# Spreading side work and reordering products around two pairs of attention outputs

## The chip, the cores and the metric

The kernel runs on one core of a Trainium2 chip. The metric is the time of one execution on the device in microseconds (us), as the median of several runs. The engines are TensorE (PE in the rows), VectorE (DVE), ScalarE (ACT), GpSimd (POOL) and SyncE (SP), which here only starts transfers.

## The reference

Four sequences `x` of 512 x 512 go through two layers. All is float32.

```python
q, k, v = x @ Wq, x @ Wk, x @ Wv
attn_out = (softmax(q @ k.T * scale) @ v) @ Wp + bp
cms_out = gelu(attn_out @ cW1 + cb1) @ cW2 + cb2 + one_hot(target_codes)
modifier = gelu(concat(attn_out, cms_out) @ mW1 + mb1) @ mW2 + mb2
x = clip(x + cms_out + modifier, 0, 1)
h = gelu(x @ W_down[stream] + b_down[stream]) @ W_up[stream] + b_up[stream]
out = layernorm(x + h) * ln_w[stream] + ln_b[stream]
```

`cW1` is 512 x 2048, `mW1` 1024 x 2048, `cW2` and `mW2` 2048 x 512. Each sequence picks one of three adapters (`W_down` 512 x 256, `W_up` 256 x 512).

## The kernel before

**Numbers in two parts.** Every matrix is split into a `hi` part (ScalarE copies it rounded) and a `lo` part (value minus `hi`, on VectorE or GpSimd), and each product is three matmuls: hi x hi, lo x hi, hi x lo (L727, L728, L729). Each matmul moves 512 columns.

**Attention** fills the first part of the time, a batch at a time. Its outputs are kept as operands: `xo[0]` for batches 0 and 1, `xo[1]` for batches 2 and 3. The two-layer perceptrons multiply 2 x 2 blocks with seven products in place of eight (the Strassen-Winograd scheme), so each pair of batches gives seven operands: the blocks `B11`, `B21`, `B22` and the sums `T1` to `T4`. Each has a `_hi`, a `_lo` and a float tile `_f` of 128 x 1024; in the trace their names are shown without the numbers, `x_B_hi`, `x_T_lo`, `x_T_f` and so on. `c_B` and `c_T` are those made from `cms_out` (`co[0]`, `co[1]`).

**Groups.** 32 groups g follow. Groups 0 to 15 are the first perceptron (`cW1`, `cW2`), with the pair of batches alternating; groups 16 (`MOD0`) to 31 are the second (`mW1`, `mW2`), 16 to 23 for batches 0 and 1, 24 to 31 for 2 and 3. A group has seven products i = 0 to 6, with operands B11, T2, T1, B21, T3, T4, B22, in three banks. Below group 16 a product has 6 matmuls; from 16 on it has 12, 6 with attention operands (`left_x`) and 6 with `cms_out` operands (`left_c`). Products 3 to 6 go on in a bank that holds an earlier one, so they wait until it has been read: product 3 for ScalarE's `keep_first` (bank 0 to `s1_t`, L1052), product 4 for VectorE's `join` U2, product 5 for U3, product 6 for JC22 (L1337). Then `gelu` (L1046) makes the four blocks C11, C22, C21, C12 of `H_hi` and `gelu_low` (L1325) those of `H_lo`. `out_tiles(g, h)` multiplies them by the second weights in four tiles of 6 matmuls each, in four further banks, and `add_outputs` (VectorE, L1348, L1352, L1354) adds these to `acc`. TensorE's order in a group g is: products 0, 1, `out_tiles(g-1, 0)`, products 2, 3, 4, `out_tiles(g-1, 1)`, products 5, 6. In group 16 it is: the attention parts of products 0, 1, 2, both `out_tiles(15, ...)`, the `cms_out` parts of 0, 1, 2, then 3 to 6. `out_tiles(g, 0)` needs `gelu_low` of C21, which the order on VectorE puts after those of C11 and C22, and `out_tiles(g, 1)` that of C12.

**Operands on their way.** `left` tiles are made from `rawX` and `rawC` (loads by SyncE, sums on GpSimd, `left_hi` on ScalarE, `left_lo` on GpSimd), `second_hi` and `second_lo` make the second weights (`W_hi`, `W_lo`, L962, L552). A left tile i is written anew after product i of the group has been made. Every engine works through its own list in order.

**Around the change.** After attention VectorE makes T2, T3, T4 of pair 1 as three differences (L1279) and, in group 0, the `lo` parts of T2, T1, T3 (L1293), while GpSimd makes those of B11, B21, T4, B22. In group 2 SyncE stores all fourteen `xo[1]` tiles of 512 KB to DRAM (L459). In groups 2 to 13 the adapters are split in 24 pieces of 128 x 256, two in each group: `split_piece` on SyncE (L412, L415) loads one, waits for the split and stores it before it goes on; ScalarE's `piece_to_hi` (L1056) stands ahead of `gelu` of C11, and a second time behind that of C22. In group 15 and 16 the `co[0]` operands are made, in 23 and 24 the `co[1]` ones (`co_sum` L1279, `co_hi` L1030, `co_lo` L1298 on VectorE and L552 on GpSimd); in group 23 `x1_home` and `cms_home` bring pair 1 back (L430, L434).

## Time and profile before

| | us |
|---|---|
| median of 3 runs | 1136.68 |
| lowest and highest | 1136.36, 1138.86 |
| the profiled execution's own time | 1140.68 |
| its span, first to last instruction | 1138.4 |
| TensorE busy in it | 1077.0 (95%) |
| mean granted TensorE clock | 0.982 of full |

The time of an execution holds 2.3 us more than its span. TensorE is busy nearly all the time; the rest of the span is its idle time, and some stretches of its busy time have a lower granted clock.

### The profile page before, as it was taken

What the parts mean: (1) busy time and instruction counts of PE and PEld (TensorE: products, weight loads), DVE (VectorE), ACT (ScalarE), POOL (GpSimd) and SP (SyncE); (2) the same over time, 40 slices, a digit from 0 to 9 for tenths busy, and PEclk for the clock granted to TensorE, in tenths of its full rate; (3) what the DMA queues carried; (4) which work ended last, traced back from release to release, by engine and by line L of the source; (5) the groups of instructions that cost most, each with busy time, mean ns of one, the idle gap of its engine ahead of it and who ended that gap; (6) DMA issues with size and microseconds to landing.
All of it is one profiled execution on the core that took longest, in us unless ns stands there. A gap on an engine that the chain in (4) does not pass through costs nothing.

```text
span 1138.4 us, 13134 instructions
## 1 busy us (share of the span) xinstructions
PE 1077.0 (95%) x4736; PEld 884.8 (78%) x4736; DVE 602.5 (53%) x831; ACT 458.2 (40%) x870; POOL 549.8 (48%) x561
## 2 busy tenths in 40 slices
PE   7999999787899999999988999999889999999996
PEld 6888888566678778778867888888678888888885
DVE  3634344562655555555663455554575455455567
ACT  3524345431433433433444333343523344332665
POOL 0501155640432422432577666666887666663414
PEclk9999999989999999999999999999989999999999
DMA  7301000107221221121041112222834212213733
GB/s 259 129 2 37 16 22 20 37 1 282 70 70 56 60 70 56 61 70 42 19 139 47 65 65 65 65 65 71 344 115 145 65 65 65 66 65 139 277 102 121
DMA packets 62064, 100.51 MB, mean 88 GB/s; under 512 B 5680, under 2 KB 35376, under 8 KB 61488
## 3 DMA queue, kind: packets, MB, share of 16 engines
q1 hardware_dynamic: 61424, 98.62, 25.3%
q10 hardware_dynamic: 576, 1.05, 0.2%
q8 instruction: 38, 0.62, 0.2%
q14 instruction: 26, 0.21, 0.1%
HBM read 77.63 MB, written 22.02 MB: 88 GB/s over the span
## 4 chain that ended last, share of the span: by engine, by line
PE 84%; DVE 7%; ACT 2%; issue 2%; SPq 2%; DMA 2%; POOL 1%; ACTq 0%; DVEq 0%
PE bank L727 28%; PE bank L728 28%; PE bank L729 28%; SPq L459 1%; DVE c_T_f L1279 1%; DVE z L1447 1%; DMA c_B_f<-cms_kept 1%; DVE x_T_lo L1293 1%; DVE stats L1441 1%; PE bank L771 1%; DVE c_T_lo L1298 1%; POOL left_c L552 1%; DMA piece_raw<-adapter_dram 0%; POOL W_lo L552 0%; ACT acc L1076 0%
## 5 line engine op out<-in xcount | busy, mean ns | idle before, releaser
L727 PE MATMUL bank<-H_hi,W_hi 128*128 128x512 f32 x512 | 201.9, 394 | 15.5 <-issue 9.3
L552 POOL TENSOR_TENSOR left_x<-rawX,left_x 128x256 fp32r<-128x256 f32 x144 | 126.5, 879 | 163.0 <-ACT left_x L957 162.7
L729 PE MATMUL bank<-H_hi,W_lo 128*128 128x512 f32 x512 | 200.9, 392 | 0.0
L728 PE MATMUL bank<-H_lo,W_hi 128*128 128x512 f32 x512 | 200.7, 392 | 0.0
L1354 DVE TENSOR_TENSOR acc<-bank,acc 128x512 f32<-128x512 f32 x224 | 151.1, 687 | 90.6 <-PE bank L729 90.2
L1337 DVE TENSOR_TENSOR u_t<-bank,s_t 128x512 f32<-128x512 f32 x64 | 44.2, 691 | 159.4 <-PE bank L729 157.3
L727 PEld LDWEIGHTS bank<-H_hi,W_hi 128*128 128x128 f32 x512 | 97.3, 190 | 38.8 <-issue 15.2
L957 ACT ACTIVATE left_x<-rawX 128x256 fp32r<-128x256 f32 x144 | 58.1, 411 | 151.2 <-DMA rawX<-mW_dram 76.8
L727 PE MATMUL bank<-x_T_hi,left_x 128*128 128x512 f32 x256 | 101.2, 395 | 12.6 <-DVE u_t L1337 11.1
L729 PEld LDWEIGHTS bank<-H_hi,W_lo 128*128 128x128 f32 x512 | 97.0, 189 | 20.7
L728 PEld LDWEIGHTS bank<-H_lo,W_hi 128*128 128x128 f32 x512 | 97.3, 190 | 20.1
L1046 ACT ACTIVATE H_hi<-u_t,bias 128x512 fp32r<-128x512 f32 x64 | 45.9, 718 | 147.7 <-PE bank L729 137.9
L729 PE MATMUL bank<-x_T_hi,left_x 128*128 128x512 f32 x256 | 100.4, 392 | 0.0
L728 PE MATMUL bank<-x_T_lo,left_x 128*128 128x512 f32 x256 | 100.4, 392 | 0.0
L552 POOL TENSOR_TENSOR piece_lo<-piece_raw,piece_hi 128x256 fp32r<-128x256 f32 x24 | 17.7, 737 | 145.0 <-ACT piece_hi L1056 145.0
L1325 DVE TENSOR_TENSOR H_lo<-u_t,H_hi 128x512 fp32r<-128x512 f32 x64 | 70.8, 1106 | 24.6 <-ACT u_t L1046 24.6
L727 PE MATMUL bank<-x_B_hi,left_x 128*128 128x512 f32 x192 | 75.7, 395 | 6.8 <-ACT gelu_f L1046 6.8
L729 PE MATMUL bank<-x_B_hi,left_x 128*128 128x512 f32 x192 | 75.4, 393 | 0.0
L728 PE MATMUL bank<-x_B_lo,left_x 128*128 128x512 f32 x192 | 75.4, 393 | 0.0
L552 POOL TENSOR_TENSOR left_c<-rawC,left_c 128x256 fp32r<-128x256 f32 x96 | 74.2, 773 | 2.4 <-ACT left_c L957 2.4
L727 PEld LDWEIGHTS bank<-x_T_hi,left_x 128*128 128x128 f32 x256 | 48.3, 189 | 25.9 <-DVE u_t L1337 13.0
L552 POOL TENSOR_TENSOR xn_lo<-x_raw,xn_hi 128x512 fp32r<-128x512 f32 x16 | 21.0, 1319 | 96.6 <-ACT xn_hi L985 96.6
(184 smaller groups left out, 2329.2 us busy)
## 6 DMA issues: line engine op xcount, KB each, us to landing
rawX<-mW_dram SPq DMA_DIRECT2D x16, 512.0 KB, 3.4
rawC<-mW_dram SPq DMA_DIRECT2D x16, 512.0 KB, 5.1
W_raw<-mW_dram SPq DMA_DIRECT2D x16, 512.0 KB, 3.7
xT_raw<-xT_dram SPq DMA_DIRECT2D x4, 1024.0 KB, 8.5
x_raw<-x_dram SPq DMA_DIRECT2D x4, 1024.0 KB, 6.4
rawX<-cW_dram SPq DMA_DIRECT2D x8, 512.0 KB, 3.6
W_raw<-cW_dram SPq DMA_DIRECT2D x8, 512.0 KB, 4.0
out_dram<-z SPq DMA_DIRECT2D x16, 256.0 KB, 2.0
```

The source lines that it names most:

```text
L459: sp.dma_start(x1_kept[i, half], f32(flat(xo[1][i][half][:, :, :]))).then_inc(x1_saved, 16)
L552: pool.tensor_tensor(dst, src, f32(hi), ALU.subtract).then_inc(done, 1)
L727: pe.matmul(tile, sh, mh, start=first_one and n == 0, stop=False, skip_group_check=joined_group)
L728: pe.matmul(tile, sh, ml, start=False, stop=False, skip_group_check=joined_group)
L729: last = pe.matmul(tile, sl, mh, start=False, stop=last_one and n == len(terms) - 1, skip_group_check=joined_group)
L771: last = pe.transpose(bank_of(n)[:, cols(c)], prob[:, t, cols(c)], ident[:, :])
L957: act.activation(left(s, i)[0], left_source(s, i), ACT.Copy).then_inc(A_hi_made[s], 1)
L1046: act.activation(dst, src, ACT.Gelu, bias=bias[:, column:column + 1]).then_inc(gelu_made, 1)
L1279: dve.tensor_tensor(dst[2][:, :, :], a, b, ALU.subtract).then_inc(done, 1)
L1325: dve.tensor_tensor(H_lo[:, c, :], f[:, :], f32(H_hi[:, c, :]), ALU.subtract).then_inc(gelu_lo_made, 1)
L1337: dve.tensor_tensor(dst[:, :], bank[b][:, :], other[:, :], ALU.add).then_inc(joined, 1)
L1354: op = dve.tensor_tensor(dst, src, dst, ALU.add)
```

## The change

- **Pair 1.** All `lo` parts of `xo[1]` move to VectorE, and none is left on GpSimd. B11's comes between the attention bias additions; T2's difference after them; T4's difference after U2 of group 0, T2's `lo` after JC22, T3's difference at the end of group 0; in group 1 the `lo` parts of T1 and B21 come between U2 and `add_outputs(0, 0)`, those of T3, T4, B22 behind it. ScalarE makes T3's and T4's `hi` between `gelu` C21 and C12 of group 0.
- **Order.** Groups 0 and 16 make product 4 ahead of product 3 (`order_of`).
- **Pieces.** One a group, in groups 3 to 26; `split_piece` is cut in `load_piece`, early in SyncE's list for the group, and `save_piece`, at its end (in group 23 it stands ahead of `x1_home(5)` and `x1_home(6)`); `piece_to_hi` and `piece_split` move to the end of the group, ahead of `second_hi` and `second_lo` there.
- **Stores.** Two of the fourteen `xo[1]` stores in each of groups 4 to 10.
- **Group 16.** All `co_lo(0, ...)` but B11 and B21 on VectorE; `add_outputs(15, ...)` earlier among them; `second_hi` right after `gelu` C11 and `second_lo` ahead of `left_lo(..., 2)`.
- **Group 24.** `co_lo(1, T2)` moves up into group 23, before `add_outputs(22, 1)`; T1's and T3's behind `add_outputs(23, 0)`.
- **Warm.** One Gelu on a 128 x 1 tile in attention's last batch.

```diff
@@ -136,6 +136,7 @@
...
+        warm = sm("warm", [1])
...
@@ -282,8 +283,11 @@
...
+        def order_of(g):
+            return (0, 1, 2, 4, 3, 5, 6) if g in (0, MOD0) else range(7)
+
         def products(g, i):
-            return 7 * g + i + 1
+            return 7 * g + list(order_of(g)).index(i) + 1
...
@@ -345,10 +349,11 @@
...
-        PIECE_GROUPS = range(2, 2 + PIECES // 2)
+        PIECE_GROUPS = range(3, 3 + PIECES)
...
         XO_HI_ORDER = (T1, T2, T3, T4)
+        XO_SUM_ORDER = [(T2, T3, T4), (T2, T4, T3)]
...
@@ -405,11 +410,13 @@
...
-            def split_piece(u):
-                e, part = u // PARTS, u % PARTS
+            def load_piece(u):
                 if u > 0:
                     sp.wait_ge(piece_saved, 32 * u)
-                sp.dma_start(piece_raw[:, :], adapter[e, part]).then_inc(piece_loaded, 16)
+                sp.dma_start(piece_raw[:, :], adapter[u // PARTS, u % PARTS]).then_inc(piece_loaded, 16)
+
+            def save_piece(u):
+                e, part = u // PARTS, u % PARTS
                 sp.wait_ge(piece_lo_made, u + 1)
                 for half, tile in enumerate((piece_hi, piece_lo)):
                     sp.dma_start(experts[e, half, :, 256 * part:256 * (part + 1)], f32(tile[:, :])).then_inc(piece_saved, 16)
@@ -452,22 +459,23 @@
...
-                if g == 2:
-                    for i in range(7):
-                        sp.wait_ge(xo_made[1][i], 1)
-                        for half in range(2):
-                            sp.dma_start(x1_kept[i, half], f32(flat(xo[1][i][half][:, :, :]))).then_inc(x1_saved, 16)
                 if g in PIECE_GROUPS:
-                    split_piece(2 * (g - 2))
+                    load_piece(g - 3)
+                if 4 <= g < 11:
+                    i = g - 4
+                    sp.wait_ge(xo_made[1][i], 1)
+                    for half in range(2):
+                        sp.dma_start(x1_kept[i, half], f32(flat(xo[1][i][half][:, :, :]))).then_inc(x1_saved, 16)
                 if g % 2 == 0 and g // 2 + 1 < 8:
                     load_second(g // 2 + 1)
                 if g in PIECE_GROUPS:
-                    split_piece(2 * (g - 2) + 1)
+                    save_piece(g - 3)
 
             for g in range(MOD0, GROUPS):
                 sets = splits_in(g)
                 if g == MOD0:
                     load_left(*sets[0])
+                    load_piece(g - 3)
...
@@ -475,10 +483,13 @@
...
                     load_left(*sets[1])
+                    save_piece(g - 3)
                     continue
                 for s, t in sets:
                     load_left(s, t)
                 load_staged(g)
+                if g in PIECE_GROUPS:
+                    load_piece(g - 3)
...
@@ -504,6 +515,8 @@
...
                 load_second(second_set(g))
+                if g in PIECE_GROUPS:
+                    save_piece(g - 3)
                 if g == 23:
                     x1_home(5)
                     x1_home(6)
@@ -633,19 +646,12 @@
...
             for op in (T3, T4):
                 xo_lo(0, op)
-            pool.wait_ge(lo_made, LAST + KT)
-            xo_lo(1, B11)
-            pool.wait_ge(xo_step[1], 3)
-            for op in (B21, T4, B22):
-                xo_lo(1, op)
...
                 if g == MOD0:
-                    co_lo(0, T4)
-                    co_lo(0, B22)
                     sums_13(*sets[0])
                     for i in (1, 2, 3):
                         left_lo(1, 0, i)
...
                     for i in (5, 6):
                         left_lo(1, 0, i)
+                    second_lo(second_set(g))
                     for i in (2, 3):
                         left_lo(*sets[0], i)
...
@@ -681,8 +688,6 @@
...
-                    if g in PIECE_GROUPS:
-                        piece_split(2 * (g - 2))
...
@@ -698,10 +703,10 @@
...
-                    if g in PIECE_GROUPS:
-                        piece_split(2 * (g - 2) + 1)
                 for s, t in sets:
                     left_lo(s, t, 5)
+                if g in PIECE_GROUPS:
+                    piece_split(g - 3)
                 if g == 23:
                     co_lo(1, T4)
                 if g == GROUPS - 1:
@@ -710,7 +715,7 @@
                             pool.wait_ge(made, products(g, 2))
                             pool.wait_ge(y01_hi_made, 2 * b + h + 1)
                             lo(y_lo[b][h][:, :, :], y01[b][:, HALF * h:HALF * (h + 1), :], y_hi[b][h][:, :, :], y01_lo_made)
-                if is_mod(g):
+                if g > MOD0:
                     second_lo(second_set(g))
...
@@ -848,19 +853,19 @@
...
-                    for i in range(3, 7):
+                    for i in order_of(g)[3:]:
...
-                for i in (0, 1):
+                for i in order_of(g)[:2]:
                     product_part(g, i, sources)
                 if g > 0:
                     out_tiles(g - 1, 0)
-                for i in (2, 3, 4):
+                for i in order_of(g)[2:5]:
                     product_part(g, i, sources)
                 if g > 0:
                     out_tiles(g - 1, 1)
-                for i in (5, 6):
+                for i in order_of(g)[5:]:
                     product_part(g, i, sources)
...
@@ -993,6 +998,7 @@
...
                         left_hi(0, 0, 0)
+                        act.activation(warm[:, :], eps[:, :], ACT.Gelu)
...
@@ -1094,15 +1100,12 @@
...
                 if g == 0:
-                    for op in (T2, T3, T4):
-                        xo_hi(1, op)
+                    xo_hi(1, T2)
...
-                if g in PIECE_GROUPS:
-                    piece_to_hi(2 * (g - 2))
...
@@ -1116,6 +1119,8 @@
...
                 gelu(g, C11)
+                if g == MOD0:
+                    second_hi(second_set(g))
...
@@ -1128,11 +1133,12 @@
...
-                if g in PIECE_GROUPS:
-                    piece_to_hi(2 * (g - 2) + 1)
                 if g == MOD0:
                     left_hi(*splits_in(g)[1], 0, g)
                 gelu(g, C21)
+                if g == 0:
+                    xo_hi(1, T3)
+                    xo_hi(1, T4)
                 if g == MOD0:
                     for i in (1, 2, 3, 4):
                         left_hi(*splits_in(g)[1], i, g)
@@ -1142,7 +1148,9 @@
                 if g == 23:
                     co_hi(1, T4)
...
+                if g in PIECE_GROUPS:
+                    piece_to_hi(g - 3)
+                if g > MOD0:
                     second_hi(second_set(g))
...
@@ -1272,30 +1280,31 @@
...
             for m in range(KT):
                 attn_f(LAST + m, B - 1, m)
-
-            def minus(dst, a, b, done):
-                dve.tensor_tensor(dst[2][:, :, :], a, b, ALU.subtract).then_inc(done, 1)
-
-            def parts(ops, op):
-                return ops[op][2][:, :, :]
-
+                if m == 1:
+                    dve.wait_ge(lo_made, LAST + m + 1)
+                    xo_lo(B11)
             dve.wait_ge(lo_made, LAST + KT)
             minus(xo[1][T2], parts(xo[1], B22), parts(xo[1], T1), xo_step[1])
-            minus(xo[1][T3], parts(xo[1], B22), parts(xo[1], T3), xo_step[1])
-            dve.wait_ge(xo_step[1], 1)
-            minus(xo[1][T4], parts(xo[1], B21), parts(xo[1], T2), xo_step[1])
...
                 dve.wait_ge(co_hi_made[q], CO_HI_ORDER[q].index(op) + 1)
-                dve.tensor_tensor(low[:, :, :], f[:, :, :], f32(hi[:, :, :]), ALU.subtract).then_inc(co_made[q][op], 1)
+                src = acc[:, 1, HALF:KT, :] if q == 0 and op == B22 else f[:, :, :]
+                dve.tensor_tensor(low[:, :, :], src, f32(hi[:, :, :]), ALU.subtract).then_inc(co_made[q][op], 1)
...
@@ -1382,24 +1391,33 @@
...
                 if g == MOD0:
-                    for op in (T4, T3):
-                        co_sum(0, op)
-                    for op in (T2, T1):
+                    co_sum(0, T4)
+                    add_outputs(g - 1, 0)
+                    co_sum(0, T3)
+                    co_lo(0, T2)
+                    add_outputs(g - 1, 1)
+                    for op in (T1, T3, T4, B22):
                         co_lo(0, op)
-                    add_outputs(g - 1, 0)
-                    co_lo(0, T3)
-                    add_outputs(g - 1, 1)
                     join(g, U2)
                 else:
-                    if g == 24:
-                        for op in (T2, T1, T3):
-                            co_lo(1, op)
                     join(g, U2)
                     if g == 0:
-                        for op in (T2, T1, T3):
+                        dve.wait_ge(xo_step[1], 1)
+                        minus(xo[1][T4], parts(xo[1], B21), parts(xo[1], T2), xo_step[1])
+                    else:
+                        if g == 1:
+                            xo_lo(T1)
+                            dve.wait_ge(xo_step[1], 2)
+                            xo_lo(B21)
+                        add_outputs(g - 1, 0)
+                    if g == 24:
+                        for op in (T1, T3):
+                            co_lo(1, op)
+                    if g == 1:
+                        for op in (T3, T4):
                             xo_lo(op)
-                    else:
-                        add_outputs(g - 1, 0)
+                        dve.wait_ge(xo_step[1], 3)
+                        xo_lo(B22)
                     if g == 24:
                         clip(0, outputs(g - 1, 0, KT - 1))
                     if g > MOD0:
@@ -1409,10 +1427,14 @@
                     co_sum(1, T2)
                 join(g, U3)
                 join(g, JC22)
-                gelu_low(g, C11)
+                if g == 0:
+                    xo_lo(T2)
+                else:
+                    gelu_low(g, C11)
                 if g == 23:
                     co_sum(1, T3)
                     co_sum(1, T4)
+                    co_lo(1, T2)
                 if g > 0 and g != MOD0:
                     add_outputs(g - 1, 1)
                 if g == 24:
@@ -1421,10 +1443,14 @@
                     co_sum(0, T1)
                     co_sum(0, T2)
                 join(g, JC21)
+                if g == 0:
+                    gelu_low(g, C11)
                 gelu_low(g, C22)
                 join(g, JC12)
+                if g == 0:
+                    minus(xo[1][T3], parts(xo[1], B22), parts(xo[1], T3), xo_step[1])
                 if g == MOD0:
-                    for op in (B11, B21, T4, B22):
+                    for op in (B11, B21):
                         dve.wait_ge(co_made[0][op], 1)
                     add_staged(g, outputs(g - 1, 1, KT - 1))
```

## Rows read from the trace of the kernel before

**Rows 1.** The page, busy time by engine: us, share, instructions.
```profile
PE 1077.0 (95%) x4736; PEld 884.8 (78%) x4736; DVE 602.5 (53%) x831; ACT 458.2 (40%) x870; POOL 549.8 (48%) x561
```

**Rows 2.** Stretches of the span: busy us and instructions by engine, clock, DMA.
```profile
240.25:260.65 20.40, 20.40 (x91) 16.89 (x90) 11.86 (x18) 8.45 (x17) 8.85 (x9) 1.00 0.00 1
...
616.51:640.99 24.48, 24.48 (x110) 20.28 (x108) 12.12 (x14) 10.71 (x22) 17.00 (x21) 1.00 0.06 22
569.00:616.51 47.51, 40.58 (x164) 32.28 (x162) 25.58 (x28) 19.77 (x39) 35.26 (x36) 0.93 0.32 111
```

**Rows 3.** TensorE's instructions behind its idle times: start, us, in brackets idle before.
```profile
222.54 0.50 PE L727 MATMUL bank<-x_T_hi,left_x 128*128 128x512 f32 x1 [2.48 <-DVE u_t L1337]
232.64 0.79 PE L727 MATMUL bank<-x_T_hi,left_x 128*128 128x512 f32 x1 [7.80 <-DVE u_t L1337]
285.32 0.80 PE L727 MATMUL bank<-x_B_hi,left_x 128*128 128x512 f32 x1 [6.83 <-ACT gelu_f L1046]
293.41 0.47 PE L727 MATMUL bank<-H_hi,W_hi 128*128 128x512 f32 x1 [2.48 <-issue]
...
505.60 0.47 PE L727 MATMUL bank<-H_hi,W_hi 128*128 128x512 f32 x1 [1.05 <-issue]
577.72 0.47 PE L727 MATMUL bank<-H_hi,W_hi 128*128 128x512 f32 x1 [3.13 <-DVE acc L1354]
609.60 0.79 PE L727 MATMUL bank<-H_hi,W_hi 128*128 128x512 f32 x1 [3.02 <-POOL W_lo L552]
828.61 0.77 PE L727 MATMUL bank<-c_T_hi,left_c 128*128 128x512 f32 x1 [8.63 <-DVE c_T_lo L1298]
```

**Rows 4.** The same view as rows 2, behind two of the idle times.
```profile
232.00:238.00 6.00, 5.36 (x15) 4.26 (x16) 3.47 (x6) 2.67 (x4) 1.26 (x2) 0.59 0.01 3
828.00:835.00 7.00, 6.39 (x17) 5.03 (x17) 6.74 (x5) 0.83 (x2) 7.00 (x3) 0.55 0.50 152
```

**Rows 5.** VectorE's instructions in order of time, from the timeline.
```profile
215.39 0.75 DVE L1203 TENSOR_SCALAR x_B_f<-bank,bias 128x512 f32<-128x512 f32 x1 [1.97 <-ACT x_B_hi L920]
...
221.81 0.68 DVE L1337 TENSOR_TENSOR u_t<-bank,s_t 128x512 f32<-128x512 f32 x1
222.41 9.57 DVE L1293 TENSOR_TENSOR x_T_lo<-x_T_f,x_T_hi 128x1024 fp32r<-128x1024 f32 x3
...
571.32 1.21 DVE L1279 TENSOR_TENSOR c_T_f<-acc 128x1024 f32<-128x1024 f32 x1
...
811.83 3.44 DVE L1279 TENSOR_TENSOR c_T_f<-c_B_f,c_T_f 128x1024 f32<-128x1024 f32 x2
815.20 2.47 DVE L1354 TENSOR_TENSOR acc<-bank,acc 128x512 f32<-128x512 f32 x4
```

**Rows 6.** SyncE's DMA instructions in order of time, first store, and what follows the last.
```profile
262.12 0.51 SPq L459 DMA_DIRECT2D x_kept<-x_B_hi  x1
...
278.48 1.21 SPq L412 DMA_DIRECT2D piece_raw<-adapter_dram  x1
```

**Rows 7.** ScalarE's instructions in order of time.
```profile
191.26 0.69 ACT L920 ACTIVATE x_B_hi<-bank,bias 128x512 fp32r<-128x512 f32 x1 [1.57 <-PE bank L729]
...
223.00 1.28 ACT L1046 ACT_TABLE_LOAD   x1
...
283.70 0.42 ACT L1056 ACTIVATE piece_hi<-piece_raw 128x256 fp32r<-128x256 f32 x1 [22.55 <-DMA piece_raw<-adapter_dram]
...
822.05 1.04 ACT L962 ACTIVATE W_hi<-W_raw 128x1024 fp32r<-128x1024 f32 x1
822.99 0.71 ACT L1046 ACTIVATE H_hi<-u_t,bias 128x512 fp32r<-128x512 f32 x1
```

**Rows 8.** GpSimd's instructions in order of time.
```profile
636.17 0.75 POOL L552 TENSOR_TENSOR left_c<-rawC,left_c 128x256 fp32r<-128x256 f32 x1
636.87 2.86 POOL L552 TENSOR_TENSOR W_lo<-W_raw,W_hi 128x1024 fp32r<-128x1024 f32 x1
...
823.90 2.34 POOL L552 TENSOR_TENSOR W_lo<-W_raw,W_hi 128x1024 fp32r<-128x1024 f32 x1
```

More of the change, by code:

```diff
@@ L946, in xo_hi @@
                 else:
-                    act.wait_ge(xo_step[q], (T2, T3, T4).index(op) + 1)
+                    act.wait_ge(xo_step[q], XO_SUM_ORDER[q].index(op) + 1)
                 act.activation(hi[:, :, :], f[:, :, :], ACT.Copy).then_inc(xo_hi_made[q], 1)
@@ L1144, in _ @@
                     co_hi(1, T1)
-                if is_mod(g):
+                if g in PIECE_GROUPS:
+                    piece_to_hi(g - 3)
+                if g > MOD0:
                     second_hi(second_set(g))
@@ L1274, in _ @@
                     lo(n, a_lo[:, m, :], tile[:, :], a_hi[:, m, :])
-            for m in range(KT):
-                attn_f(LAST + m, B - 1, m)
             def minus(dst, a, b, done):
```

11 lines of the change are left out of this document (7 added, 4 removed).

## The prediction

> **What bounds the kernel now.** I read the page's busy times first: TensorE is busy for 95% of the span [rows 1], so another engine counts only where TensorE waits for it. The stretches come next. A group below 16 takes 20.40 us when nothing is late, for 90 matmuls, so 0.2267 us for one, 1.36 us for six (a short product, or one source of a long one, or a tile of `out_tiles`) and 5.44 us for four tiles [rows 2]. Then TensorE's timeline, for each instruction ahead of which it sat idle [rows 3]: 2.48 and 7.80 us in group 0, 6.83 at the start of group 3 and 2.48 before its `out_tiles`, small ones up to 505.60, 3.13 and 3.02 us around group 16, 8.63 in group 24. An idle time costs more than itself: behind that of 7.80 us the granted clock is 0.59 over 6 us, and behind the 8.63 us it is 0.55 over 7 us; the lower of the two levels (half, 1.2 of 2.4 GHz) holds for 4 to 6 us there, so 2 to 3 us are lost [rows 4]. I take a loss of 1.4 to 1.9 us behind idle times of 3 to 4.5 us, since the mean clock over the 47.51 us with two such idle times is 0.93, 3.3 us in all [rows 2].
>
> **Stores and the first piece (group 3).** SyncE issues fourteen stores between 262.12 and 278.48, 16.4 us, and only then the first piece's load [rows 6]. ScalarE's `piece_to_hi` waits 22.55 us for it at 283.70, with `gelu` C11 queued behind it [rows 7], and TensorE's group 3 waits for that gelu [rows 3]. From `out_tiles` at 260.65 to the next group's at 293.41 there are 32.76 us, less 20.40: 12.4 us lost [rows 2, 3]. After the change the first load stands in group 3 and is wanted at that group's end, over 15 us later, and two stores (1.2 us each) stand in a group where SyncE otherwise waits. The order of the transfers leaves nothing in the way: gain 12.4.
>
> **Two pieces a group.** From 293.41 to 505.60 there are ten groups and 212.19 us, less 204.0: 8.2 us [rows 2, 3]. They go with the pieces: 1.05 to 2.5 us in each even group, where a piece's copy sits ahead of `gelu` C21. Moved behind C21, a late piece delays only C12, whose `out_tiles` comes 8 us later. Gain 8.2.
>
> **What the pieces cost in groups 17 to 26.** Each puts 0.3 to 0.4 us on ScalarE ahead of `second_hi`, and a 256-column operation on GpSimd, 0.70 us by the pitch of such operations, ahead of `second_lo` [rows 7, 8]. `W_lo` ended at 639.73 and `out_tiles` began at 640.99 [rows 2, 8], so 1.26 us of room become 0.5: cost nothing; if the cover were gone, 0.7 us a group.
>
> **Groups 0 and 1.** TensorE's group 0 starts at 214.47 (`out_tiles` in group 1 at 240.25, which is 25.78 us later; 54 matmuls are 12.24): 13.5 us are lost now. VectorE does three differences and three `lo` parts between its joins U2 and U3, the latter in 9.57 us, 3.2 each, beside GpSimd's long operations; alone such an operation is 1.21, beside short ones 1.72 [rows 5]. Now step by step. VectorE's last bias addition ends at 216.14, T2's difference at 217.4, U2 starts then, and TensorE can use it 0.73 us later (221.81 to 222.54) [rows 3, 5], at 218.2; product 4, now fourth, is due at 218.55. With it ahead of product 3, U3 and JC22 are in time too, and group 0 ends at 224.0. Then VectorE is the slower: C11 and C22 `lo` to 224.7, JC12 to 225.3, T3's difference to 226.5, C21's `lo`, so `out_tiles(0, 0)` begins at 227.35 in place of 226.7: 0.65 lost. ScalarE now makes T3 and T4 `hi` (2.0 us, 1.04 for such a copy) before `gelu` C12 (two of 0.71) and `keep_first` [rows 7], so U2 of group 1 ends only at 231.2. T1's `lo` at 1.72 ends at 232.9 (due 232.8), B21's at 234.5 (due 234.4), four evictions take 2.5 [rows 5], T3's `lo` ends at 238.5 where product 4 is due at 235.9. That is 0.65 + 0.3 + 2.7, with 0.8 for the clock behind it 4.5 us lost. Gain 13.5 - 4.5 = 9.0. At 1.21 for every `lo` it would be 10; at 3.2 for every one, T3's ends at 243 and the gain is 3.
>
> The table load of 1.28 us [rows 7] leaves this chain, and is in these times. It goes ahead of the copy at 191.26, before which ScalarE idles for 1.57: with a small Gelu of up to 0.7 it makes that copy 0.4 late, and its bank is wanted only several tiles on: nothing. The Trainium skill (ScalarE: Activation LUTs, What ACT_TABLE_LOAD costs) gives a drain of about 1.38 us with every load, 2.66 together; by that the copy were 1.8 late, still under cover, and the sum would not move.
>
> **Group 16.** The 3.13 us go: `add_outputs(15, 0)` comes before T3's difference, so the banks are free in time. From 569.00 eight tiles (10.88) and three `cms_out` parts (4.08) bring TensorE to 584.0. But product 4 comes first now and needs U2, and VectorE puts four `lo` parts ahead of it. They can start after the last eviction at 580.7, and GpSimd has its queue of short operations then, so 1.72 each [rows 5]: 587.6, and TensorE goes on at 588.3, 4.3 us late. This idle time replaces the old. Two products and 1.9 for the clock end at 595.6. The second change there, `second_lo` brought forward, makes GpSimd wait for `gelu` C11 of the product now fifth: two gelus and the copy of `W_hi` (2.5), `W_lo` (2.4), four short operations (2.8), and three more until the first `left_c` of group 17 (2.1) end at 605.4. TensorE wants it after two products and a part at 602.4: 3.0 late. With its 4.08 us of parts and products, 5.44 of tiles and 1.4 for the clock the tiles end at 616.3, against 616.51 now [rows 2]. Gain 0.2: the wait for `W_lo` becomes one for `left_c`. If VectorE's four run at 1.21 each, U2 comes 2 us sooner; if they run at 3.2, 6 us later. Range -4 to +5.
>
> The Trainium skill (SBUF — State Buffer, Who interferes with whom) says that a VectorE operation with two SBUF inputs and a GpSimd one that reads SBUF lock each other out for a whole instruction, and this speaks against the move. By it VectorE waits at most for one short operation, 0.75, so 1.96 each and 1.0 us more than by the row.
>
> **Groups 23 and 24.** The wait of 8.63 us is for T2's `lo`, which now comes early. But the weights stand next in the way: `W_lo` ended at 826.24 (823.90 + 2.34) [rows 8] and `out_tiles` began at 831.3, six slow matmuls (0.427 each) after 828.61 [rows 3, 4]. Ahead of it are now T2's `lo` on VectorE before JC21 (1.72), 0.45 for the piece's load in SyncE's list, 0.3 on ScalarE, and on GpSimd the piece (0.70) waiting for ScalarE ahead of `co_lo(1, T4)` (2.35). I get the piece at 824.6 to 825.3, T4 at 827.6, `W_lo` at 830.2: the tiles start 1.0 earlier than now. They run at the half clock for about 5 us, end at 838.3, and only then come the last eviction and T1's `lo`: product 2's second part begins at 840.8 and ends at 842.1, where it ends at 840.9 now. Loss 1.2 (range -4 to +4: with no piece in the way 3 better, with 3.2 us for T1 and T2 3 worse).
>
> **Sum.** 12.4 + 8.2 + 9.0 + 0.2 - 1.2 = 28.6 us; I take off 0.4 for small lateness: 28.2. The profiled execution took 1140.68, 2.3 more than its span, and becomes 1112.5. The median of the runs shown is 4.0 lower than that execution; the same gain from 1136.68 gives 1108.5.
>
> **The rivals.** (a) Groups 16 and 24 do gain: the four `lo` parts find GpSimd idle and the late waits shrink, 5 us more, 1103.5. For it: 1.21 alone is measured. Against: GpSimd is busy for 35.26 of the 47.51 us there [rows 2]. 15%. (b) Contention on VectorE in groups 0, 1, 16 and 24 is 3.2 us an operation [rows 5]: 6 to 9 us less, about 1116. Against: GpSimd's long operations are gone from there but `W_lo`. 17%. (c) The change doesn't do what it says for the pieces: ScalarE still waits for each, since a load must wait until the store before has landed, and the 8.2 us stay: 1117. Against: save and load now lie most of a group apart. 6%. (d) Slower: the room of 0.5 us at `W_lo` in groups 17 to 26 goes. If a piece comes late, ScalarE's `second_hi`, GpSimd's `second_lo` and `out_tiles` follow. It needs 2.8 us a group, ten times, to eat 28; at 4 us it is 1149. Against: the load is queued a whole half group before. 3%. My forecast has 59%.
>
> **How the numbers follow.** About 0.2%, 2.3 us, is what a measurement can tell from no change. The forecast's own range is 1106 to 1112. To leave no more than 2 in 10 out it reaches to (a) and most of (b): 1103 to 1116. Slower has (d), 3%; within 0.2% another 2%; faster 95%.
>
> **What would show it.** Right: no idle time of TensorE from group 2 to 15, `piece_to_hi` with no DMA wait; in group 1 an idle time of 2 to 3 us before product 4; in group 16 one of 4 us behind U2, then one of 3 us behind `left_c` in group 17; in group 24 about 7 us ahead of `out_tiles(23, 0)`, released by `W_lo`, and about 2 us before group 24's second product behind JC21. Wrong would be: `W_lo` releasing TensorE in groups 18 to 27, more than 4 us before product 4 of group 1, or neither stall around group 16.

## The result, and the profile after

| | before | changed |
|---|---|---|
| median of 4 runs each, on one chip | 1137.77 us (1136.36 to 1140.13) | 1110.90 us (1110.41 to 1112.28) |
| ratio | | 0.9758, 95% interval 0.9738 to 0.9778 |
| profiled span | 1138.4 us | 1110.5 us |
| mean granted clock of the span | 0.982 | 0.991 |

The change makes the kernel 26.9 us faster by the medians and 27.9 us by the two profiled spans. The forecast was 28.2 us and 1108.5 us, with a range of 1103 to 1116.

The page of the changed kernel, busy times by engine, beside [rows 1]:

```profile
PE 1071.2 (96%) x4736; PEld 882.9 (80%) x4736; DVE 593.6 (53%) x837; ACT 454.8 (41%) x871; POOL 538.1 (48%) x555
```

TensorE does the same 4736 matmuls. It is busy 5.8 us less, although nothing was taken from it: that is the clock, which stays up longer. The remaining 22 us are idle time that is gone. VectorE has six instructions more and GpSimd six fewer: the `lo` parts that moved.

TensorE's instructions behind its idle times in the changed kernel (start, us, in brackets the idle before), beside [rows 3]:

```profile
238.12 0.47 PE L732 MATMUL bank<-x_T_hi,left_x 128*128 128x512 f32 x1 [2.40 <-DVE x_T_lo L1293]
...
556.73 0.50 PE L732 MATMUL bank<-x_T_hi,left_x 128*128 128x512 f32 x1 [3.49 <-DVE u_t L1346]
...
575.02 0.79 PE L732 MATMUL bank<-c_B_hi,left_c 128*128 128x512 f32 x1 [4.14 <-POOL left_c L565]
...
790.74 0.50 PE L732 MATMUL bank<-x_T_hi,left_x 128*128 128x512 f32 x1 [1.78 <-DVE s_t L1346]
...
800.80 0.79 PE L732 MATMUL bank<-H_hi,W_hi 128*128 128x512 f32 x1 [7.02 <-POOL W_lo L565]
...
811.50 0.47 PE L732 MATMUL bank<-c_T_hi,left_c 128*128 128x512 f32 x1 [0.78 <-DVE c_T_lo L1307]
```

The large idle times of [rows 3] are gone: `W_lo` is still a releaser, but in group 24 in place of 16, and T2's `lo` part, which held group 24 for 8.63 us, holds nothing; T1's does, for 0.78. Between 240 and 535 us nothing over 0.3 us is left. The six above are what the change leaves or makes; there are two more, 0.43 at 535.27 and 1.09 at 780.50.

The path can be cut at the starts of `out_tiles`, since TensorE does the same matmuls in every stretch (the one called group 16 below begins at `out_tiles(14, 1)`, in group 15). In each cell of the table the first number is the time from one such start to the next and the one in brackets is the sum of TensorE's idle times over 0.3 us in it. What differs beyond the brackets is matmuls at the lower clock and shorter idle times.

| stretch | before | changed | gained | forecast |
|---|---|---|---|---|
| start of `out_tiles(0, 0)` | 240.25 | 227.03 | 13.2 | 12.85 (13.5 less 0.65) |
| to `out_tiles(1, 0)` | 20.40 | 23.41 (2.40) | -3.0 | -3.85 |
| to `out_tiles(2, 0)` | 32.76 (10.34) | 20.40 (0) | 12.4 | 12.4 |
| to `out_tiles(14, 1)` | 262.61 (6.83) | 254.32 (0) | 8.3 | 8.2 |
| to the end of `out_tiles(16, 0)` | 60.49 (7.36) | 60.96 (8.06) | -0.5 | +0.2 |
| to `out_tiles(22, 0)` | 174.08 (0) | 174.08 (0) | 0 | 0 |
| to `out_tiles(23, 1)` | 55.75 (8.63) | 58.20 (10.67) | -2.45 | -1.2 |
| to the end of the last `out_tiles` | 242.08 (0) | 242.08 (0) | 0 | 0 |

The gains add to 27.9. (Group 0 itself starts at about the same time in both, so the first line is what group 0 no longer loses.) Rows of single stretches of the changed kernel, by windows (busy us and instructions by engine, clock, DMA share, GB/s):

```profile
227.03:270.84 43.81, 41.41 (x181) 33.71 (x181) 31.12 (x40) 17.75 (x32) 14.89 (x12) 1.00 0.08 27
525.16:586.12 60.96, 52.90 (x217) 42.51 (x216) 38.56 (x43) 24.65 (x50) 42.91 (x44) 0.94 0.24 83
760.20:818.40 58.20, 47.53 (x194) 37.78 (x192) 31.14 (x34) 22.43 (x42) 46.34 (x43) 0.91 0.62 229
```

PE's busy time and the idle time add to the first stretch exactly (41.41 + 2.40 = 43.81). The last of the three holds the most of what is still lost: a stretch that would take 43.52 us at the pace of groups 17 to 21 (29.92 for a whole group, 13.60 from its first `out_tiles` to its second) takes 58.20, of which 10.67 are idle and 4.0 the lower clock.

### The profile page after: what moved, and what is told of

The parts are those of the page before. It is cut to its first block, busy times and chain, and to the rows that moved or that the text cites. A ratio compares the mean times of both kernels' runs of the same rounds, so it can differ in the third digit from the quotient of the medians.

```text
span 1110.5 us, 13134 instructions
## 1 busy us (share of the span) xinstructions
PE 1071.2 (96%) x4736; PEld 882.9 (80%) x4736; DVE 593.6 (53%) x837; ACT 454.8 (41%) x871; POOL 538.1 (48%) x555
## 4 chain that ended last, share of the span: by engine, by line
PE 87%; DVE 6%; POOL 2%; ACT 2%; DMA 1%; issue 1%; SPq 0%; DVEq 0%; ACTq 0%; POOLq 0%
PE bank L732 29%; PE bank L733 29%; PE bank L734 29%; DVE z L1473 1%; DMA c_B_f<-cms_kept 1%; DVE stats L1467 1%; DVE c_T_f L1284 1%; POOL W_lo L565 1%; PE bank L776 1%; POOL left_x L565 1%; DVE c_T_lo L1307 0%; ACT acc L1082 0%; DMA WqT_raw<-WqT_dram 0%; DVE H_lo L1334 0%; DVE acc L1363 0%
## 5 line engine op out<-in xcount | busy, mean ns | idle before, releaser
L1334 DVE TENSOR_TENSOR H_lo<-u_t,H_hi 128x512 fp32r<-128x512 f32 x64 | 73.3, 1145 | 42.0 <-ACT u_t L1052 42.0
L565 POOL TENSOR_TENSOR piece_lo<-piece_raw,piece_hi 128x256 fp32r<-128x256 f32 x24 | 22.8, 951 | 106.9 <-ACT piece_hi L1062 106.9
```

The source lines that it names most:

```text
L565: pool.tensor_tensor(dst, src, f32(hi), ALU.subtract).then_inc(done, 1)
L1334: dve.tensor_tensor(H_lo[:, c, :], f[:, :], f32(H_hi[:, c, :]), ALU.subtract).then_inc(gelu_lo_made, 1)
```

## The experiments

Each kernel ran four times beside the kernel before. They were measured in three sets, each on one chip, on which the kernel before had medians of 1138.5 us (the first four experiments), 1139.8 (the next four) and 1140.3 (the last four). So the ratio is the measure between sets (0.0010 is 1.1 us; its interval is ±0.0016 to ±0.0022, most of it the spread of the kernel before), and the medians are one within a set. The changed kernel ran in none of the three sets: where a median below is given as so much under it, the ratios say 0.5 to 1.7 us more: 5.6 us for `order_g0_only`, 5.1 for `u2_early`, 7.5 for `w_before_c11`, 2.8 for `w_first_g23`, 3.2 for `t3_early_g1`, 3.1 for `skip_pieces`. The last four columns are the stretches of the table above, from one profiled execution of each kernel; that of the changed kernel is its slowest of four, 1.4 us over its median.

| kernel | median us | ratio | `out_tiles(0, 0)` to `(2, 0)` | `(2, 0)` to `(14, 1)` | group 16 | groups 22 to 24 |
|---|---|---|---|---|---|---|
| before | 1137.77 | 1 | 53.16 (10.34) | 262.61 (6.83) | 60.49 (7.36) | 55.75 (8.63) |
| changed | 1110.90 | 0.9758 | 43.81 (2.40) | 254.32 (0) | 60.96 (8.06) | 58.20 (10.67) |
| pieces_only | 1123.67 | 0.9872 | 40.80 (0) | 254.32 (0) | 62.57 (8.21) | 57.45 (10.52) |
| no_pieces_change | 1130.69 | 0.9926 | 57.34 (12.26) | 262.59 (6.75) | 60.65 (8.23) | 56.35 (8.77) |
| order_g0_only | 1105.86 | 0.9709 | 43.85 (2.40) | 254.32 (0) | 56.23 (4.39) | 57.15 (10.73) |
| order_g16_only | 1114.03 | 0.9783 | 45.41 (2.39) | 254.32 (0) | 60.49 (8.01) | 57.43 (10.94) |
| u2_early | 1106.26 | 0.9713 | 43.81 (2.40) | 254.32 (0) | 56.41 (4.57) | 56.42 (7.99) |
| w_before_c11 | 1104.88 | 0.9692 | 43.85 (2.38) | 254.32 (0) | 55.22 (3.89) | 57.47 (10.15) |
| w_first_g23 | 1108.88 | 0.9733 | 43.85 (2.40) | 254.32 (0) | 62.31 (8.04) | 52.80 (6.84) |
| t3_early_g1 | 1108.82 | 0.9730 | 42.27 (0.47) | 254.32 (0) | 61.93 (8.03) | 56.14 (9.53) |
| skip_pieces | 1109.48 | 0.9731 | 45.46 (2.38) | 254.32 (0) | 61.93 (8.01) | 52.93 (7.21) |
| all_swapped | 1099.97 | 0.9644 | 42.24 (0.47) | 254.32 (0) | 54.73 (3.52) | 55.16 (7.20) |
| all_natural | 1099.72 | 0.9647 | 42.26 (0.47) | 254.32 (0) | 54.56 (4.38) | 50.86 (4.63) |
| all_swapped_skip | 1097.87 | 0.9629 | 42.28 (0.48) | 254.32 (0) | 54.68 (3.52) | 52.21 (5.78) |

**Pieces and stores alone, and all but them.** `pieces_only` is the kernel before with the new piece and store schedule; `no_pieces_change` is the changed kernel with the old one.

```diff
-        PIECE_GROUPS = range(2, 2 + PIECES // 2)
+        PIECE_GROUPS = range(3, 3 + PIECES)
...
-                if g == 2:
-                    for i in range(7):
...
+                if 4 <= g < 11:
+                    i = g - 4
```

> The kernel before with only the piece and store parts of the change. My theory: the 12.4 us of group 3 and the 8.2 us of the even groups go in full and nothing else moves, but the piece in group 23 sits ahead of the second weights there; 20.6 less and 0.5 to 1 back, so 1117 to 1118, and no idle time of TensorE between group 2 and group 15. Rival: these waits only hide others (second weights or left tiles late), then half or less of it, 1127 or more.

Measured: 1123.67 us, ratio 0.9872 (0.9851 to 0.9892): 14.8 us, where I expected over 19. The table shows that the gain did come: groups 1 and 2 lose nothing (53.16 becomes 40.80), groups 2 to 14 take 254.32, together 20.7. It was partly given back: 2.1 in group 16 and 1.7 in groups 22 to 24, which makes 16.9, the difference of the profiled spans (1121.5 against 1138.4). My expectation had 0.5 to 1 for group 23 and nothing for group 16. No run moved the stores without the pieces, so how the 20.7 divide between the two rests on the places where they arise in the trace.

> The changed kernel with the old two pieces a group and the fourteen stores in group 2. My theory: parts are independent, so what is left is groups 0 and 1 (10 us by the trace after), group 16 (-0.5) and group 24 (-2.5, of which 1 to 1.5 is the piece's and goes away here): 1129 to 1131. Rival: the stores and pieces work against the moved lo parts, then the sum of this gain and that of the piece parts alone is off from 27 us by more than 3.

Measured: 1130.69 us, ratio 0.9926 (0.9905 to 0.9948), as expected. By the profiled spans the halves sum to 16.9 + 9.1 = 26.0 us, and both together give 27.9. By the medians they sum to 14.8 + 7.8 = 22.6 against 26.9, further off than the 3 us that the rival asks for; but each of these gains has an interval of about ±2.4 us, so the runs don't decide whether the halves help each other. In the profiles the difference of 1.9 lies in group 16, while those of the other stretches cancel: the pieces cost 2.1 there with the old order and the other edits 0.2, and together they cost 0.5.

**The two product orders.** Each is the changed kernel with the new order in one group alone; the diff is that of `order_g0_only`, the other has `g == MOD0` there.

```diff
-            return (0, 1, 2, 4, 3, 5, 6) if g in (0, MOD0) else range(7)
+            return (0, 1, 2, 4, 3, 5, 6) if g == 0 else range(7)
```

> The changed kernel with product 4 ahead of product 3 only in group 0; group 16 in the natural order. My theory: the new order makes TensorE wait for U2 behind four lo parts while product 3 could run. Without it the idle time of 3.5 us in group 16 falls below 1, gelu C11 and with it the weights and the left tiles of group 17 come some 5 us sooner, and the idle time of 4.1 us shrinks to about 1: 4 to 7 us faster than the changed kernel, 1104 to 1107. Rival: the order is needed there for U3 as in group 0: equal or up to 2 us slower, 1111 to 1113.

Measured: 1105.86 us, ratio 0.9709 (0.9689 to 0.9730): 5.0 us under the changed kernel's median. Group 16 takes 56.23 in place of 60.96: the wait of 3.49 for U2 gives way to two of 0.76 and 0.78 behind VectorE's joins, and `left_c` is 2.42 late in place of 4.14. So the new order there is a loss of 4.7 us in the company of the rest of the change, and its near zero in the forecast's table (-0.5) is a loss of 4.7 set off against a gain of 4.3 that the other edits bring (60.49 to 56.23).

> The changed kernel with product 4 ahead of product 3 only in group 16; group 0 in the natural order. My theory: U3 of group 0 can start only after product 4, one product later, and every step of VectorE behind it up to C21's lo shifts by about as much: 1 to 1.5 us slower than the changed kernel, 1112 to 1112.5, and about 0.9 us of idle time before product 5 of group 0. Rival: VectorE's work behind it is what counts and U3 is not on its path: no difference, 1111.

Measured: 1114.03 us, ratio 0.9783 (0.9763 to 0.9804), 3.1 over the changed kernel; more than the 1 to 1.5 that my theory had, though the two ratio intervals overlap. In the profile `out_tiles(0, 0)` starts at 228.45 in place of 227.03, behind idle times of 0.78 and 0.33: 1.4, as expected. Then the same wait in group 1 costs 1.6 more (45.41 against 43.81, idle 2.39 and 2.40): the clock, of which more below. That the order caused this part too is not shown.

**The two waits of group 16.** The forecast put the first down to U2 behind four `lo` parts, the second to GpSimd waiting for `W_hi`, which ScalarE holds behind `gelu` C11. VectorE and GpSimd of the changed kernel, in order of time:

```profile
549.81 4.60 DVE L1307 TENSOR_TENSOR c_T_lo<-c_T_f,c_T_hi 128x1024 fp32r<-128x1024 f32 x3
554.33 1.74 DVE L1307 TENSOR_TENSOR c_B_lo<-acc,c_B_hi 128x1024 fp32r<-128x1024 f32 x1
555.99 0.68 DVE L1346 TENSOR_TENSOR u_t<-bank,s_t 128x512 f32<-128x512 f32 x1
```

```profile
564.11 0.69 ACT L1052 ACTIVATE H_hi<-bank,bias 128x512 fp32r<-128x512 f32 x1 [5.33 <-PE bank L734]
564.70 0.68 ACT L1052 ACTIVATE gelu_f<-bank,bias 128x512 f32<-128x512 f32 x1
565.27 1.06 ACT L967 ACTIVATE W_hi<-W_raw 128x1024 fp32r<-128x1024 f32 x1
```

```profile
566.40 2.41 POOL L565 TENSOR_TENSOR W_lo<-W_raw,W_hi 128x1024 fp32r<-128x1024 f32 x1 [6.35 <-ACT W_hi L967]
...
574.24 0.72 POOL L565 TENSOR_TENSOR left_c<-rawC,left_c 128x256 fp32r<-128x256 f32 x1
```

```diff
-                    for op in (T1, T3, T4, B22):
-                        co_lo(0, op)
+                    co_lo(0, T1)
                     join(g, U2)
+                    for op in (T3, T4, B22):
+                        co_lo(0, op)
```

> The changed kernel with one edit in group 16: U2 is formed by VectorE right behind the first co_lo, ahead of those for T3, T4 and B22. Theory: the 3.5 us in which TensorE has no ready product (556.7 us of the changed kernel's span) is the time that U2 is late behind three evictions of 4.6, 1.8 and 1.0 us; with U2 early it goes, and about 4 to 4.5 us with the slow-clock time behind it, unless the next wait, for left_c at 575 us (4.1 us), grows by what is won. So between 1106.5 us (the gap goes) and 1110.5 us (the left_c wait takes it all, if left_c hangs on ScalarE's own order and not on the product). Rival: the evictions pushed behind U2 make a later product wait, and the time stays at 1110 to 1112.

Measured: 1106.26 us, 4.6 under the changed kernel, ratio 0.9713 (0.9696 to 0.9731). The idle time behind U2 is gone and that for `left_c` is still 4.14. It did not grow, because C11's product came earlier too and took GpSimd's whole chain forward: `left_c` is there at 569.8 and not 575.0. So this wait hangs on the product, by way of the gelu.

```profile
569.87 0.80 PE L732 MATMUL bank<-c_B_hi,left_c 128*128 128x512 f32 x1 [4.14 <-POOL left_c L565]
```

```diff
+                if g == MOD0:
+                    second_hi(second_set(g))
                 gelu(g, C11)
-                if g == MOD0:
-                    second_hi(second_set(g))
```

> The changed kernel with one edit in group 16: ScalarE evicts the second pair's W_hi ahead of the gelu of C11's product. Theory: the wait of 4.1 us for left_c at 575 us comes from W_hi waiting 5.3 us in ScalarE's queue behind an operation that waits for a later product, so it goes and brings 4 to 5 us: 1105.5 to 1107 us. Rival: left_c waits for GpSimd's own queue (6.4 us idle ahead of W_lo is then not the cause), and the time stays at 1110 to 1111; or the gelu, now later, holds C11's next product and half comes back, 1108 to 1109.

Measured: 1104.88 us, 6.0 under the changed kernel, ratio 0.9692 (0.9676 to 0.9708). Group 16 takes 55.22 in place of 60.96. The wait for `left_c` is gone: `W_hi` is copied at 558.75, and GpSimd follows at once.

```profile
558.75 1.04 ACT L967 ACTIVATE W_hi<-W_raw 128x1024 fp32r<-128x1024 f32 x1
564.18 0.69 ACT L1052 ACTIVATE H_hi<-bank,bias 128x512 fp32r<-128x512 f32 x1 [4.40 <-PE bank L734]
```

```profile
558.68 1.43 POOL L565 TENSOR_TENSOR left_c<-rawC,left_c 128x256 fp32r<-128x256 f32 x2
560.06 2.39 POOL L565 TENSOR_TENSOR W_lo<-W_raw,W_hi 128x1024 fp32r<-128x1024 f32 x1
```

**The wait for `W_lo` in group 24.** GpSimd and ScalarE of the changed kernel ahead of `out_tiles(23, 0)` at 800.80:

```profile
794.95 0.72 POOL L565 TENSOR_TENSOR piece_lo<-piece_raw,piece_hi 128x256 fp32r<-128x256 f32 x1 [0.88 <-ACT piece_hi L1062]
795.63 2.36 POOL L565 TENSOR_TENSOR c_T_lo<-c_T_f,c_T_hi 128x1024 fp32r<-128x1024 f32 x1
797.94 2.80 POOL L565 TENSOR_TENSOR W_lo<-W_raw,W_hi 128x1024 fp32r<-128x1024 f32 x1
```

```profile
792.58 1.99 ACT L1036 ACTIVATE c_T_hi<-c_T_f 128x1024 fp32r<-128x1024 f32 x2
794.47 0.40 ACT L1062 ACTIVATE piece_hi<-piece_raw 128x256 fp32r<-128x256 f32 x1
794.78 1.04 ACT L967 ACTIVATE W_hi<-W_raw 128x1024 fp32r<-128x1024 f32 x1
```

GpSimd could go on at 794.07 but waits for the piece's `hi`, behind two copies on ScalarE: 0.88 + 0.68 is what the piece costs it directly. Two edits, one that puts `W_hi` and `W_lo` first, one that takes the pieces out of groups 16 and 23:

```diff
                 if g == 23:
+                    second_hi(second_set(g))
                     co_hi(1, T4)
                     co_hi(1, T1)
                 if g in PIECE_GROUPS:
                     piece_to_hi(g - 3)
...
+                if g == 23:
+                    second_lo(second_set(g))
                 if g in PIECE_GROUPS:
                     piece_split(g - 3)
```

```diff
-        PIECE_GROUPS = range(3, 3 + PIECES)
+        PIECE_GROUPS = [g for g in range(3, 5 + PIECES) if g not in (MOD0, 23)]
```

> The changed kernel with one edit in group 23: the second pair's W_hi and W_lo are issued ahead of T4's eviction and of the adapter piece on ScalarE and GpSimd. Theory: the 7.0 us idle ahead of out_tiles(23,0), released by W_lo, is a queue of piece_lo (0.9 us), c_T_lo (2.4 us) and W_lo (2.8 us) on GpSimd, so W_lo lands some 3 to 4 us earlier and 3.5 to 5 us are won with the clock: 1106 to 1107.5 us. Rival: T4, which then is 3 to 4 us later, stops the product that reads it as long as W_lo did, and the time is the same within 1 us.

Measured: 1108.88 us, 2.0 under, ratio 0.9733 (0.9717 to 0.9750). The wait for `W_lo` fell from 7.02 to 2.68, that for T1's `lo` grew from 0.78 to 2.37, and groups 22 to 24 take 52.80 in place of 58.20. The rival's T4 stopped nothing: T1's `lo` starts behind `add_outputs(23, 0)` and takes 2.93 us there, beside two 128x1024 operations of GpSimd, where it took 1.34 in the changed kernel with only short ones beside it. But group 16, which the edit does not touch, takes 62.31 in place of 60.96, with the same idle times.

```profile
796.57 0.80 PE L734 MATMUL bank<-H_hi,W_hi 128*128 128x512 f32 x1 [2.68 <-POOL W_lo L565]
...
807.34 0.47 PE L734 MATMUL bank<-c_T_hi,left_c 128*128 128x512 f32 x1 [2.37 <-DVE c_T_lo L1310]
```

```profile
801.38 4.73 POOL L565 TENSOR_TENSOR c_B_lo<-c_B_f,c_B_hi 128x1024 fp32r<-128x1024 f32 x2
...
804.26 2.93 DVE L1310 TENSOR_TENSOR c_T_lo<-c_T_f,c_T_hi 128x1024 fp32r<-128x1024 f32 x1
```

> The changed kernel with no adapter piece in groups 16 and 23; the pieces behind them move on by one and by two groups (3 to 15, 17 to 22, 24 to 28). Theory: the piece in group 23 stands in the queues ahead of W_hi and W_lo and costs about 1.85 us at out_tiles(23,0) (the stretch from out_tiles(22,0) to out_tiles(23,1) is 58.2 us in the changed kernel and 56.35 us with the old pieces), and the one in group 16 costs 0 to 1 us there: together 1108 to 1109 us. Rival: the late W_lo is T4's eviction alone and group 16 does not see its piece, so the time stays at 1110.5 to 1111.3 us.

Measured: 1109.48 us, ratio 0.9731 (0.9715 to 0.9748): 1.4 under by the medians, of another chip, and 3 by the ratio, so the size is open between them. In the trace the wait for `W_lo` is 5.00 in place of 7.02 and GpSimd does T4's `lo` at 794.40, straight behind the short operation; `W_lo` itself took 2.34 in place of 2.80, which with the 0.88 and 0.68 makes the 2.02. In group 16 the idle times are the same without a piece (8.01 and 8.06). So in the changed order a piece costs about 2 us of waiting in group 23 and nothing in group 16; that `pieces_only` lost 2.1 there belongs to the old order, where `W_hi` stands right behind the piece's copy and its `W_lo` released TensorE 3.61 late, where it was 3.02 [rows 3]. Of the 2.1 only 0.85 are idle time (8.21 against 7.36); the rest is the clock.

**T3's low part in group 1.**

```diff
                             xo_lo(B21)
+                            xo_lo(T3)
                         add_outputs(g - 1, 0)
...
-                        for op in (T3, T4):
-                            xo_lo(op)
+                        xo_lo(T4)
```

> The changed kernel with one edit in group 1: VectorE evicts T3's low part ahead of add_outputs of group 0. Theory: the 2.4 us idle at 238 us is x_T_lo late behind the output additions, so it goes: 1108 to 1108.8 us. Rival: add_outputs is late instead and holds the output's banks, which stops TensorE for as long in out_tiles(1,0); 1110 to 1111.5 us.

Measured: 1108.82 us, ratio 0.9730 (0.9714 to 0.9746), 2.1 under. The 2.40 us are gone, 0.47 came at 248.20, and the stretch takes 42.27 in place of 43.81. The rival's late banks can be there only as that 0.47, whose releaser the trace doesn't name.

The intervals of the ratios of `w_first_g23`, `skip_pieces`, `t3_early_g1` and `order_g16_only` overlap with that of the changed kernel (0.9738 to 0.9778). For the first three the idle times of the traces carry the reading, and the gain in time is some 1 to 3 us. Those of `order_g0_only`, `u2_early` and `w_before_c11` lie below it.

**Together.**

> The changed kernel with all four edits that won: U2 early and W_hi ahead of C11's gelu in group 16, W_hi and W_lo first in group 23, T3's low part early in group 1. Theory: the four waits are separate places of the path, so the times won add: 4.6, 6.0, 2.0 and 2.1 us make 14.7, so 1096 us, 1095 to 1098. Rival: with U2 early the products of group 16 come 4 us sooner, and the operands behind them (left_c, W_lo) become the next wait, so that the two edits of group 16 bring only some 6 to 7 us together: 1100 to 1101 us.

> The changed kernel with group 16 in the old product order, W_hi and W_lo first in group 23, and T3's low part early in group 1. Theory: the times won add, 5.0 by the order of group 16, 2.0 and 2.1 us: 1101.8 us, 1101 to 1103. If the order of group 16 is worth having once its waits are gone, all_swapped is some 5 us under this one; rival: both end within 1 us of each other, as GpSimd's queue sets group 16 in either order.

> all_swapped and no pieces in groups 16 and 23. Theory: what skip_pieces wins over the changed kernel is won here too in group 16 alone, since in group 23 the piece no longer stands ahead of W_lo: 0 to 1 us under all_swapped. Rival: the piece in group 23 now holds T4 instead, which is then what the second wait of group 24 hangs on, and all of it (1.9 us and more) comes back: 2 to 3 us under all_swapped.

Measured, on one chip: 1099.97, 1099.72 and 1097.87 us (ratios 0.9644, 0.9647 and 0.9629). The four edits of `all_swapped` bring 10.9 us by the medians and 13.0 by the ratios, where their single gains sum to 14.7 and 18.6: they overlap. Group 16 shows where: alone, U2 early wins 4.6 us there and `W_hi` early 5.7, together 6.2, since `left_c` is late again by 3.09 once the products come earlier. `all_natural` has group 16 in the old order and neither of that group's two edits, and it reaches the same time: the new order with its two edits brings nothing over the old one without them (54.73 against 54.56), and the rival held, with `left_c` from GpSimd the last wait of group 16 in both (3.09 and 2.42). No run has the old order with `W_hi` early, so what the order alone is worth then is open. (The last stretch of `all_natural` has one idle time of 1.65, behind `W_lo` of group 24.) Taking the two pieces out of their groups wins 2.1 more, in the trace all of it in groups 22 to 24 (55.16 to 52.21), so the rival of `all_swapped_skip` held in size. In kind it is shown only in part. The waits fall by 1.42: 0.67 at T1's `lo` on VectorE and not at T4, since without the piece GpSimd's long operations beside it end sooner, 0.8 us behind its start in place of 1.5 (it takes 1.90 in place of 2.57); 0.73 is a wait behind `cms_kept` that comes and goes without any piece (see below). The remaining 1.5 are the clock. That kernel is the fastest, 3.7% under the one before (0.9613 to 0.9645).

## Why the prediction was right, and where its terms were off

**Stores and first piece, 12.4: shown.** Measured 12.4 in the changed kernel and, with only pieces and stores changed, in `pieces_only` (53.16 to 40.80). No `piece_to_hi` waits for a load in the changed kernel.

**Two pieces a group, 8.2: shown.** 8.3; it comes back when the old pieces do (262.59 in `no_pieces_change`).

**Groups 0 and 1, 9.0: 10.2 measured, the step on group 1 was too dear.** `out_tiles(0, 0)` begins at 227.03, forecast 227.35: T3's difference runs at 225.11 and 1.22 us, and C21's `lo` follows at 226.25. The wait before product 4 is 2.40, forecast 2.7. The 0.8 for the clock did not come: over the stretch behind this wait the clock is 1.00. Of the edits behind this gain only the order (`order_g16_only`) and T3's place (`t3_early_g1`) were tried alone; that the rest comes from the moved differences, `lo` parts and table load is read from the rows, not shown by a run.

```profile
238.12:249.00 10.88, 10.88 (x48) 9.04 (x49) 10.05 (x13) 3.47 (x7) 4.50 (x4) 1.00 0.00 1
```

The table load did no harm ahead of the copy, which starts at 191.14, where it was at 191.26 [rows 7]:

```profile
189.59 1.28 ACT L1001 ACT_TABLE_LOAD   x1
190.89 0.20 ACT L1001 ACTIVATE warm<-eps 128x1 f32<-128x1 f32 x1
191.14 0.69 ACT L925 ACTIVATE x_B_hi<-bank,bias 128x512 fp32r<-128x512 f32 x1
```

The Trainium skill (ScalarE: Activation LUTs, What ACT_TABLE_LOAD costs) adds a drain of about 1.38 us to such a load. Here the small Gelu starts 0.02 us behind the load's 1.28, and no row shows a drain.

**Group 16, +0.2: -0.5 measured; both waits came.** The first is 3.49 for 4.3 forecast, since the four `lo` parts took 6.3 us and not 6.9; the second is 4.14 for 3.0, since among GpSimd's seven operations behind `W_lo` three took 1.17 to 1.19 and not 0.7. Their sum is 7.6 against 7.3. `u2_early` and `w_before_c11` show both causes as named. The Trainium skill (SBUF — State Buffer, Who interferes with whom) has the two engines lock each other out, by which the four were 1.0 us more than my figure; they took 0.6 less.

**Groups 23 and 24, -1.2: -2.45 measured, the largest miss among the terms.** The step was "the piece at 824.6 to 825.3, T4 at 827.6, `W_lo` at 830.2: the tiles start 1.0 earlier than now". The order and the releaser are right, but TensorE's tiles started only 0.1 earlier. From the start of `out_tiles(22, 0)` the forecast has the piece from 34.0 to 34.7, T4's end at 37.0 and `W_lo`'s at 39.6; the changed kernel has the piece from 34.75 to 35.47, T4's end at 37.79 and `W_lo`'s at 40.54. So the chain starts 0.75 late; `W_lo` adds the rest, since it ran for 2.80, where the row of before had 2.34. What sets the chain back is an idle time of 1.09 at 780.50, which the forecast put at nothing: TensorE waits for U2, and on VectorE U2 stands behind a sum that waits for a `cms_kept` tile to come back.

```profile
776.74 1.77 DVE L1284 TENSOR_TENSOR c_T_f<-c_T_f,c_B_f 128x1024 f32<-128x1024 f32 x1 [7.74 <-DMA c_B_f<-cms_kept]
```

This wait is not steady (0 to 1.19 over the kernels), and the start of the tiles goes with it in the six kernels that have this group as the changed one has it, both counted from `out_tiles(22, 0)`:

| | u2_early | t3_early_g1 | w_before_c11 | order_g0_only | changed | order_g16_only |
|---|---|---|---|---|---|---|
| wait for U2 | 0 | 0 | 0.31 | 0.74 | 1.09 | 1.19 |
| start of `out_tiles(23, 0)` | 39.53 | 39.75 | 39.81 | 40.23 | 40.60 | 40.67 |

Before, the tiles started at 40.72. Where the wait is absent they start 1.0 to 1.2 earlier, as forecast, and the stretch takes 56.14 (`t3_early_g1`) or 56.42 (`u2_early`), 0.4 to 0.7 over the 55.75 of before. So the step that was missing is this wait. What makes the tile come at varying times is open. The wait for JC21 (1.78, forecast 1.72) came as well, and T1's `lo` holds the next product by 0.78. What the piece does is shown twice: without it the wait for `W_lo` is 5.00 in `skip_pieces` and 4.99 in `no_pieces_change`.

**The rivals.** (a) Groups 16 and 24 did not gain. (b) In group 24 two `lo` parts took 3.02 together, beside short operations of GpSimd, and the four of group 16 6.3; none took 3.2. It is not gone for good: in `w_first_g23` one took 2.93 and in `all_natural` one took 3.40, beside GpSimd's 128x1024 operations. (c) No piece stopped TensorE in groups 3 to 14: twelve and a half groups of 20.40 without idle time. (d) In group 18 `W_lo` ends at 639.96 and the tiles begin at 640.52: the room of 0.5 is 0.56 and it held in the other groups with a piece, since the stretches of groups 17 to 22 and from 24 on are the same as before, 174.08 and 242.08 us.

**Small lateness, -0.4** was not needed. **The sum:** against the profiled spans the terms were off by +1.2 (groups 0 and 1), +0.1, -0.7 (group 16), -1.25 (groups 23 and 24) and +0.4. They nearly cancel, so that 28.2 and 27.9 lie as close as 0.3 is luck; that every one of these terms came within 1.3 us is not. **Median against span:** the forecast took the median to lie 4.0 below the profiled execution in both kernels. The changed kernel's profiled execution took 1112.28 (forecast 1112.5), 1.8 more than its span, and its median lies only 1.4 below it. That is where the 2.4 us between 1108.5 and 1110.90 come from.

## What to carry to other kernels

Cut the path at one repeated point of the engine that bounds it, and book each edit in its own stretch. The stretches of two profiles then add up to the difference of the spans, and an edit that loses 4.7 us in the shade of one that wins 4.3 is seen. When a product is moved forward, list for every in-order engine what stands ahead of its operand (here U2 behind four evictions, `W_hi` behind a gelu of a product that had just been moved back). Two waits in a row on one chain don't add: the second edit wins only what the next late operand leaves.

## What the runs showed of the hardware

**The same wait costs different amounts.** In group 1 TensorE idles 2.38 to 2.40 us in eight of the kernels of the table, which differ little ahead of it. In five of them the next `out_tiles(1, 0)` comes 23.41 to 23.45 us behind `out_tiles(0, 0)`, in `skip_pieces`, `order_g16_only` and `no_pieces_change` 25.01 to 25.06. In `skip_pieces` the granted clock is 0.84 there, in the changed kernel 1.00:

```profile
237.40:248.00 10.60, 10.53 (x39) 8.59 (x40) 8.49 (x10) 1.75 (x3) 4.54 (x4) 0.84 0.00 1
```

Group 16 shows it too: with the order and the idle times alike (8.01 to 8.06), it takes 60.49 to 62.31 us. Against 43.52 us and the idle time, groups 22 to 24 lose 2.2 (`skip_pieces`) to 4.9 us (`u2_early`) by the clock. What decides it is open: no run varied the moment of a wait alone, and one execution of each kernel was traced, while the executions of one kernel differ too (the kernel before, in the last set, had one span of 1137.0 us at a mean clock of 0.983 and one of 1139.1 at 0.978). For readers it means that a trace settles 1 to 2 us of an edit only by its idle times, not by the length of the stretch behind them.

**VectorE beside GpSimd.** A 128x1024 `lo` part took 1.21 to 1.22 us alone and 1.53 to 1.76 beside short GpSimd operations. Beside two long ones of GpSimd it took 2.93 us in `w_first_g23`, and the next, behind their end, 1.21 again. GpSimd's 256-column operation took about 0.73, 1.18 or 1.72 us.
